# Three graph attention layers on one core: own products earlier in a chunk, the row of G earlier, one running maximum, DVE's steps on the sums later

## The reference

```
h = x @ W
e = leaky_relu((h @ a_src)[src] + (h @ a_dst)[dst], 0.2)
e = exp(e - segment_max(e, dst)[dst])
out = segment_sum(h[src] * (e / segment_sum(e, dst)[dst])[:, None], dst) + b
```

## Time and profile before

| | us |
|---|---|
| median of 3 runs | 688.24 (688.14 to 689.72) |
| profiled execution | 687.7 |
| its span (first to last instruction) | 686.0 |
| DVE busy in the span | 639.8 |
| PE busy | 587.9 |
| ACT busy | 484.7 |
| POOL busy | 459.6 |

### The profile page before, as it was taken

The page is one execution under the profiler, slowest core; times in us unless marked ns, Lnnn a source line. Parts: engine busy times, 40 slices in busy tenths (PEclk is TensorE's granted clock), DMA queues, the critical chain, the costliest instruction groups (busy, mean ns, idle before and its releaser), DMA issues.

```text
span 686.0 us, 13824 instructions
## 1 busy us (share of the span) xinstructions
PE 587.9 (86%) x5571; PEld 570.1 (83%) x5571; DVE 639.8 (93%) x911; ACT 484.7 (71%) x719; POOL 459.6 (67%) x448
## 2 busy tenths in 40 slices
PE   1728845989869899999999979999989989999995
PEld 1628744988769899989999979899989979999994
DVE  3999979999999989999987999999998899999994
ACT  0416543655969787887765878989886698898891
POOL 5579103589908656675954775858598688697883
PEclk9959977899999899999999999999999999999998
DMA  2410002000000000000100100000010010110001
GB/s 69 119 56 2 1 9 38 1 2 1 20 1 1 20 1 20 1 1 9 20 20 1 27 1 20 1 19 2 8 20 20 1 27 3 37 29 11 20 1 42
DMA packets 22325, 12.07 MB, mean 18 GB/s; under 512 B 12393, under 2 KB 20055, under 8 KB 22255
## 3 DMA queue, kind: packets, MB, share of 16 engines
q1 hardware_dynamic: 21455, 9.85, 6.2%
q0 software_dynamic: 800, 1.26, 0.6%
HBM read 9.47 MB, written 1.64 MB: 16 GB/s over the span
## 4 chain that ended last, share of the span: by engine, by line
DVE 52%; PE 28%; issue 8%; DMA 6%; POOL 4%; ACT 1%; POOLq 0%; DVEq 0%; SPq 0%
PE ps L1813 21%; DVE scratch L951 21%; DVE ps L1067 16%; DVE scratch L1149 5%; DMA xr<-in_x 3%; POOL scratch L751 2%; DVE ps L1069 2%; DVE ps L1079 1%; PE ps L1866 1%; PE ps L1821 1%; DMA gathered<-ext_lines 1%; PE ps L1844 1%; DVE scratch L1067 1%; DMA gathered<-in_edges,start_i 1%; DMA ext_lines<-ext 1%
## 5 line engine op out<-in xcount | busy, mean ns | idle before, releaser
L1813 PE MATMUL ps<-hB,scratch 125*125 125x129 f32 x3450 | 404.7, 276 | 21.3 <-DVE scratch L1149 17.8
L1813 PEld LDWEIGHTS ps<-hB,scratch 125*125 125x125 f32 x3450 | 390.7, 189 | 28.6 <-DVE scratch L1149 23.0
L751 POOL TENSOR_TENSOR scratch<-scratch,C 125x625 f32<-125x625 f32 x239 | 304.1, 1283 | 124.1 <-ACT scratch L1569 122.1
L1067 DVE SCALAR_TENSOR_TENSOR ps<-C,a_unit,ps 125x625 f32<-125x625 fp8e3 x330 | 275.5, 867 | 2.3
L1567 ACT ACTIVATE scratch<-gathered,r_neg 125x625 f32<-125x625 f32 x219 | 176.6, 806 | 18.7 <-PE ps L1813 17.5
L1569 ACT ACTIVATE scratch<-scratch,r_src 125x625 f32<-125x625 f32 x219 | 179.0, 817 | 7.1
L1452 ACT ACTIVATE C<-ps 125x1000 fp8e3<-125x1000 f32 x80 | 78.0, 1000 | 78.5 <-PE ps L1780 78.3
L1780 PE MATMUL ps<-scratch 128*128 128x125 bf16 x1250 | 90.3, 235 | 40.0 <-DVE scratch L951 38.1
L1780 PEld LDWEIGHTS ps<-scratch 128*128 128x128 bf16 x1250 | 83.0, 105 | 46.8 <-DVE scratch L951 44.7
L1149 DVE SCALAR_TENSOR_TENSOR scratch<-ps,r_src,C 125x625 f32<-125x625 f32 x121 | 104.2, 861 | 4.2 <-PE ps L1803 4.1
L951 DVE TENSOR_TENSOR scratch<-key_lo,ps 128x4096 bf16<-128x4096 bf16 (+3 forms) x41 | 89.8, 2190 | 0.0
(11 more groups left out here) (195 smaller groups left out, 451.5 us busy)
## 6 DMA issues: line engine op xcount, KB each, us to landing
gathered<-g_lines SPq DMA_DIRECT2D x15, 305.2 KB
xr<-in_x SPq DMA_DIRECT2D x1, 1562.5 KB
out<-xr SPq DMA_DIRECT2D x4, 312.5 KB
edge_sb<-in_edges SPq DMA_DIRECT2D x1, 805.7 KB
gathered<-ext_lines SPq DMA_DIRECT2D x5, 122.1 KB
w<-in_W SPq DMA_DIRECT2D x2, 128.0 KB
out<-xr SPq DMA_DIRECT2D x1, 187.5 KB
out<-xr SPq DMA_DIRECT2D x1, 125.0 KB
```

What stands on the lines that cost most here:

```text
L751: g.tensor_tensor(slot[s], slot[s], C5[:, q % NC, s, :], ALU.mult).then_inc(pool_done, 1)
L1067: v.scalar_tensor_tensor(dest, counts, unit[:, s:s + 1], top, ALU.min, ALU.max).then_inc(S.top_done, 1)
L1813: last = mm(ps[0:P, acc_at(t):acc_at(t) + HW], A[:, P * t:P * (t + 1)], feat, start=opens and t in (0, 3), stop=closes, skip_group_check=True)
```

## The change

- `OWN` and a new `INNER` in place of `ODD` with `MORE`: DVE's own blocks stand earlier in a chunk; their number per chunk stays (4, 9, 7, 11, 12, then 10 and in layer 3 nine). The turns keep their blocks.
- `rows_at`: the row of G two blocks after DVE's last own block (at most 23), save in the chunk ahead of a turn.
- One running maximum at `TOP0`; `in_odd`, `join_tops` and what waits for them are gone.
- `USUAL`: `chain`, `kappa`, `z` and `stats` one to three blocks later; what POOL, PE and ACT do after them stays where it was. Of `USUAL`, the second entry is for chunks 6 to 8, the third for 11 to 14.
- `EXT_AT`, `OVER_AT`, `EXPS_AT`: 14, 15, 16 become 15, 17, 18; so the blocks of chunk 0 stand between tiles 22 and 35 instead of 20 and 35.

```diff
-        OWN = ((), (15, 18, 20, 22), (1, 4, 7, 10, 13, 15, 18, 20, 22), (1, 5, 9, 13, 16, 19, 22), (0, 2, 4, 7, 10, 12, 14, 16, 18, 20, 22))
+        OWN = ((), (13, 15, 17, 19), (0, 2, 4, 7, 9, 11, 13, 15, 17), (1, 3, 5, 8, 11, 14, 17), (0, 2, 4, 6, 8, 10, 12, 14, 15, 16, 18))
...
-        EXT_AT = FEAT_AT[-1] + 2
-        OVER_AT = EXT_AT + 1
+        EXT_AT = FEAT_AT[-1] + 3
+        OVER_AT = EXT_AT + 2
...
-        MORE = (0, 6, 12, 18, 22)
+        INNER = ((0, 1, 2, 4, 6, 8, 10, 12, 14, 16), (1, 2, 4, 6, 8, 10, 12, 14, 16))
...
-        USUAL = (At(1, (3, 4, 5, 6), 6, (8, 9, 10), None, (14,), (12, 15, 21), (14, 17, 23), 18, 20),
-                 At(1, (2, 2, 3, 3), 4, (4, 4, 4), (9, 9), (11, 15), (15, None, 17), (14, 16, 19), None, None),
-                 At(1, (3, 4, 5, 6), 6, (8, 9, 10), None, (14, 17, 20), (None,) * 3, (None,) * 3, None, None))
+        USUAL = (At(1, (5, 6, 7, 8), 7, (10, 11, 12), None, (14,), (12, 15, 21), (14, 17, 23), 18, 20),
+                 At(1, (4, 4, 5, 5), 5, (6, 6, 6), (10, 10), (11, 15), (15, None, 17), (14, 16, 19), None, None),
+                 At(1, (5, 6, 7, 8), 7, (10, 11, 12), None, (14, 17, 20), (None,) * 3, (None,) * 3, None, None))
...
-            if q < NC:
-                return ODD
             if turn(q):
                 return tuple(sorted(ODD + TURN_MORE))
-            return tuple(sorted(ODD + MORE[(1 if q < 2 * NC else 0):]))
+            return tuple(s for s in range(T) if s not in INNER[q // NC - 1])
...
         def rows_at(q):
-            return 23 if turn(q) else 22
+            return 22 if q % NC == NC - 1 else min(23, max(s for s in range(T) if s not in POOL_OF[q]) + 2)
...
-                n = q * (T + 1)
-                odd = in_odd(s, q if S is F else None)
-                at_ = TOP1 if odd else TOP0
-                top = ps[0:P, at_:at_ + CD]
-                same = [k for k in range(s) if in_odd(k, q if S is F else None) == odd]
-                if same:
-                    dve.wait_ge(S.top_done, n + same[-1] + 1)
-                elif q:
+                n = q * T + s
+                top = ps[0:P, TOP0:TOP0 + CD]
+                if n:
                     dve.wait_ge(S.top_done, n)
-                if s == LAST_ODD and q:
+                if s == T - 1 and q:
                     dve.wait_ge(S.top_T, q)
-                dest = top_a if s == LAST_ODD else top
-                if same:
+                dest = top_a if s == T - 1 else top
+                if s:
...
-            def join_tops(S, q):
-                dve.wait_ge(S.top_done, q * (T + 1) + T)
-                v.tensor_tensor(top_a, top_a, ps[0:P, TOP0:TOP0 + CD], ALU.max).then_inc(S.top_done, 1)
```

More of the change, by code:

```diff
@@ L441, in post_at @@
             return TURN[L] if turn(q) else BEFORE_LAST[L] if q % NC == NC - 1 and L < 2 else USUAL[L]
-        def in_odd(k, q=None):
-            if q in (1, 2):
-                return k % 2 == 1 and not any(at_ == AFTER and (c, k) == (q, k_) for at_, c, k_ in FIRST_TOPS[q])
-            return k >= AHEAD and k % 2 == 1
-        LAST_ODD = max(k for k in range(T) if in_odd(k))
-        def tops_before_rows(q):
-            if q in (2, 3):
-                c, k = min((c, k) for at_, c, k in FIRST_TOPS[q - 1] if at_ == AFTER)
-                return c * (T + 1) + k
-            return q * (T + 1) if q > 1 else 0
         def top_at(q, k):
@@ L459, in top_at @@
             return (k - AHEAD) * (T - 3) // (T - 1 - AHEAD)
-        def join_at(q):
-            return top_at(q, T - 1) if turn(q) else top_at(q, T - 1) + 1
         def rows_at(q):
-            return 23 if turn(q) else 22
+            return 22 if q % NC == NC - 1 else min(23, max(s for s in range(T) if s not in POOL_OF[q]) + 2)
         def pool_no(q, s):
@@ L1162, in first_tops @@
                         next_top(c, k)
-                        if k == T - 1:
-                            join_tops(F, c)
             def chunk(q):
@@ L1178, in chunk @@
                                 next_top(q, k)
-                        if s == join_at(q):
-                            join_tops(F, q)
                     if q:
@@ L1371, in careful_chunk @@
                     top_step(K, a_unit[0], q, i)
-                join_tops(K, q)
                 for part in range(3):
@@ L1784, in top_transpose @@
             def top_transpose(S, q):
-                pe.wait_ge(S.top_done, (q + 1) * (T + 1))
+                pe.wait_ge(S.top_done, (q + 1) * T)
                 if q:
@@ L1800, in fast_rows @@
                 for t in range(CT):
-                    if t == CT - 1 and q > 1:
-                        pe.wait_ge(F.top_done, tops_before_rows(q))
                     last = tr(ps[0:P, ROWU + 128 * t:ROWU + 128 * t + P],
```

## The result

The changed kernel takes **704.65 us** (median of 4 runs, 704.17 to 706.63) where the kernel before took 688.19 us beside it (4 runs, 687.9 to 689.72): a ratio of 1.0241, 95% interval 1.0223 to 1.0258, slower. The forecast was 696.0 us with a range to 700.0. The direction was right, the size was half of the true one: +8.3 us against the profiled execution, where +16.5 came, and the range missed it.

What follows compares the result with a forecast made beforehand. The prediction took DVE to set the pace, with PE following and bounding part of layer 1. It summed 687.7 - 3.4 + 4.8 - 0.4 + 1.4 + 5.9 = 696.0 us, range 688.0 to 700.0 us.

Steps and rivals of the forecast that it cites:

- Count stage, -3.4: Reduction over the extremes: a second tile of one-hots covers DVE's 3.39 us wait for the DMA, saving 3.4 us.
- fourth rival: Count stage: POOL ends its first 25 blocks over 3 us later than counted, the 3.4 us are repaid: 699.4 us; chance 0.09.
- One running maximum, +6.2 us of DVE: Chunks 1 to 14: 125 more same-sum waits of 0.13 us outweigh 14 joins of 0.72 us saved, net +6.2 us.
- third rival: Running-maximum steps cost 0.775 us whatever they follow, so layers 2 and 3 gain: 684.2 us; chance 0.07.
- Layer 1, +4.8: Chunks 1 to 3, up to chunk 5: PE idles before block 13, loses its clock and delays DVE; +4.8 us, between +1.5 and +6.5.
- The wait of 2.98 us in chunk 2 gives back about 2.5: Layer 1, chunk 2: DVE's existing wait of 2.98 us absorbs about 2.5 us of the lateness.
- Layer 2, -0.4: DVE gains some 0.33 us in each turn behind the attention terms and nothing else: -0.4 us.
- That the row of G is made sooner is worth nothing: Making the row four to five blocks sooner gains nothing, as maxima precede each chunk's first product and no middle chunk waits.
- Layer 3, +1.4: Chunks 11 to 13: DVE's own sum grows by 0.4, 0.5 and 0.5 us, together +1.4 us.
- The end, +5.9: Chunk 14: rz and POOL's scaling come later, with nine POOL blocks instead of seven behind; +5.9 us, from +2.5 to +6.5.
- The second: Rival: DVE's lead pays, PE sets the period and 8.9 us of its gaps in chunks 6 to 9 go: 681.6 us; chance 0.06.
- The fifth: Rival: no lost clock in chunk 1 (+1.5) and only two more blocks at the end (+2.5): 689.3 us; chance 0.18.

Runs made afterwards that it cites:

- m2_ext_later: Kernel before with only the reduction over the extremes moved to two tiles behind their write instead of one: 685.6 us, ratio 0.9951.
- m1_one_max: Kernel before with only the second running maximum and its joins taken out, all steps on one maximum: 693.08 us, ratio 1.0071.
- m3_own_first: Kernel before with only DVE's own blocks earlier in a chunk; two maxima, late row of G, old steps on the sums: 705.13 us, ratio 1.0228.
- o1_two_maxima: Kernel before with every part of the change except the single running maximum and the sooner row of G: 706.72 us, ratio 1.0255.
- n2_rows_back: Changed kernel with the row of G back at block 22 of every chunk (23 in a layer's first): 710.82 us, ratio 1.031.
- n4_inner_back: Changed kernel with DVE's blocks in the inner chunks of layers 2 and 3 at their old places, row of G at block 23: 700.24 us, ratio 1.0157.
- n6_kappa_psum: Changed kernel where layer 3 first copies kappa's five columns into PSUM, so the z0 step reads one operand from there: 703.66 us, ratio 1.0208.
- n1_steps_back: Changed kernel with the steps on the sums, kappa and POOL's scaling of layers 2 and 3's inner chunks at their old blocks: 705.29 us, ratio 1.0218.
- n5_last_chunk_back: Changed kernel with DVE's own blocks back at their old places in chunk 14 alone: 700.57 us, ratio 1.0167.
- m4_steps_later: Kernel before with only the steps on the sums one to three blocks later (chunks 6 to 8 and 11 to 14): 693.06 us, ratio 1.0058.

## Why the prediction was right or wrong

- **Count stage, -3.4: right.** m2_ext_later measures -3.4, and the fourth rival (first blocks too late) did not come.
- **One running maximum, +6.2 us of DVE: right.** m1_one_max gives +4.9 us of time. The 182 pairs of neighbouring steps that both read the same sum in the changed kernel start 0.909 us apart on average, against the 0.905 of the earlier trace rows. The third rival falls.
- **Layer 1, +4.8: right in chunk 1, wrong behind it; 7.3 were measured.** The terms as listed add up to 4.3 (4.6 + 0.7 - 2.5 + 0.6 + 1.2 - 0.3), so 0.5 of the 4.8 has no source. Chunk 1 gave +5.2 against 5.3, with the stall, the low clock and the reduction where they were forecast. Two steps failed. "The wait of 2.98 us in chunk 2 gives back about 2.5": with the 0.6 that the second half of that chunk was to add, 1.9 us were to come back and 0.6 did. And "0.3 us of PE's stalls in chunk 4 go": by PE's starts the chunk became 1.25 us longer. PE's waits in it grew by 0.5 us (a wait of 0.32 for a product of DVE went, 0.56 for one of POOL's and 0.26 for ACT came); the rest I cannot place. A third step came out by luck. Chunk 3 became 1.2 us longer by PE's starts (38.3 to 39.6), as forecast for the held products 8, 11 and 14, but with the own products moved alone (m3_own_first) it takes 38.3 us as before, and with one maximum alone (m1_one_max) 39.3. So most of it is the single maximum's. The trace shows the same: PE's waits for DVE's products grew by 0.4 us there, and that for ACT's move of the sums by 0.55 (0.80, before 0.26).
- **Layer 2, -0.4: wrong by 1.7 us.** "And nothing else" was the step that failed. The inner chunks 6 to 8 together gained 1.1 us. But PE now runs 3.16 us behind DVE at the starts of chunks 7 to 9, 1.95 before, and DVE waits 1.14 us for the transposes in chunk 9, whose steps the change leaves at the old blocks (`BEFORE_LAST`), and 0.92 us in chunk 10; the two chunks cost 2.4 us more than before. The cost of chunk 9 needs the sooner row too: with own blocks first and the row late (m3_own_first, o1_two_maxima, n2_rows_back) PE is 1.95 us behind and the chunk takes 34.4 to 34.6 us, against 35.8. That of chunk 10 comes with layer 2's own blocks first, whatever the row, and goes with them (n4_inner_back). Later steps in chunk 9 were not tried.
- **"That the row of G is made sooner is worth nothing": wrong as a term.** I read it from the kernel before, where maxima stand ahead of a chunk's first product. The same change puts products first. In the changed kernel taking the row back costs 4.8 us (n2_rows_back). It was counted at nothing, and the stall it avoids was not counted either, so this error cost the sum little; it did make the expectation of m3_own_first miss.
- **Layer 3, +1.4: wrong by 2.8 us, the largest single miss of mechanism.** The single maximum costs 1.3 there (m1_one_max), as said. The step that failed is that I priced the moved steps on the sums only by what comes late behind them, not by what they meet in their new place: L1086 inside a POOL product, 0.69 us longer in each chunk, 2.1 us in chunks 11 to 13 and 0.7 in chunk 14. n6_kappa_psum and n1_steps_back show it from two sides. The rest, some 0.8 us, is put to the own blocks first: taking them back (n4_inner_back) gives 1.0 us in chunks 11 to 13.
- **The end, +5.9: right in mechanism, 1.2 short.** `rz` came 17.3 us behind DVE's first product of the chunk (656.99 to 674.25), where 16.1 were forecast, 0.7 of the difference by L1086. Two more blocks of POOL were priced at 2.5; putting the old order back gives 4.0 us (n5_last_chunk_back). The rest of the 7.1 I put to the lateness: the later steps alone add 2.2 (m4_steps_later).
- **The rivals.** The second (DVE's lead pays) is refuted as a whole, PE's waits for DVE's products rose from 17.8 to 25.3 us. The fifth needed an unchanged clock in chunk 1 and only two blocks at the end; both failed. The list of DVE's waits also left out 0.80 us in chunk 3 and 3.95 us ahead of the last reduction; no term of the sum rests on them. None of the rivals held a second cost in layer 3 or a PE lag in layer 2, so the range, built from them and my own terms, ended at 700: layer 1 (2.5 us), layer 2 (1.7), layer 3 (2.8) and the end (1.2) were each short, and all in one direction.

## What to carry to other kernels

Price a moved instruction twice: by who waits for its result, and by what the other engines do at the time it will now run; a five-element step can cost 0.7 us because of its neighbour. Split a change with several parts before judging it, since one part (here the count stage, -3.4 us) can be good inside a whole that is bad, and another (the sooner row) can promise nothing in the kernel before, where no inner chunk waits for it, and be worth 4.8 us in company. And do not copy the order of the inner chunks to the last one: where nothing follows, work handed to the front only leaves the slower engine alone at the end, 4.0 us here.
